# The prologue of a transformer decoder block: loads on two queues, products of ones at the start, v made between the first maximum scores

## The chip, the cores and the metric

The kernel runs on one core of one Trainium2 chip. A core has TensorE (matrix products), VectorE, ScalarE and GpSimd, and SyncE, which here only issues transfers; each takes its own instructions in order, and they meet at semaphores. A transfer can be issued by SyncE, ScalarE or GpSimd and runs on 16 shared DMA engines. The metric is the device time of one execution in microseconds (us), the median of several.

## The reference, cut to what matters

```python
def attn(x, w_q, w_k, w_v, w_o):              # x: 4 x 1024 x 256, 16 heads of 16
    q, k, v = x @ w_q.T, x @ w_k.T, x @ w_v.T # split into heads
    scores = einsum("bqhd,bkhd->bhqk", q, k) * 16 ** -0.5
    return (softmax(scores) @ v) @ w_o.T
x = layernorm(x + attn(x, ...))
x = layernorm(x + cross_attn(x, ctx, ...))    # 77 context rows, one head of 256
x = layernorm(x + moe(x, ...))                # 8 experts 256 -> 1024 -> 256, top 2
```

All is float32. The change touches only the beginning of the first line: q, k and v of batch 0.

## The kernel before

The whole block is one program. Self-attention is done head by head, 64 heads in all (4 batches of 16). For each head there are 8 tiles of 128 rows, and each tile is scored twice: once with the rows across the partitions, to get each row's maximum (`score_max`, into the banks pa; VectorE reduces it in `maxima`), and once turned round, with the negated maxima as three more rows of the contraction, so that ScalarE can take the exponential straight from PSUM (`score_exp`, `exponentials`). The main loop runs over 256 pairs of tiles (`for p in range(PAIRS)`); the maxima run LEAD = 8 pairs, that is two heads, ahead of the exponentials. Side work for the layers behind is spread over the same loop by its number. After it come 71 tiles of the expert layer. The order on each engine is written out by hand, as one stream of instructions for each.

Products with q and k are done in bf16, so each of q and k is split into three bf16 parts, high, middle and low: ScalarE rounds (`first_high`), VectorE subtracts (`first_remainder`), ScalarE rounds again (`first_middle`), VectorE subtracts again (`first_low`). The parts go to DRAM (`store_group`, three transfers for a group) and come back by head, stacked to 96 rows (`load`, three transfers for q and three for k).

The prologue, before the main loop, runs so:
- SyncE issues w_q, w_k, four pieces of x (two column halves, two row halves), w_v, all on its queue.
- TensorE waits for both weights and the first half of x, then makes 8 groups of q and k (`project_qk`, 512 columns each, in the order q, k of column half 0, q, k of half 1, for the first eight heads, and the same for the last eight), then v in 8 products of 256 columns (`project_v`), then 16 maximum scores (heads 0 and 1), then it enters the main loop.
- SyncE stores groups 0 to 3 as their parts come, waits until these have landed, issues twelve loads for heads 0 and 1, stores groups 4 to 7, loads head 2 and x of the next batch, and then sends the negated maxima of head 0 to DRAM (`store_neg`) and back as rows of q's tile (`load_rows`).
- VectorE sets constants (the semaphore set_up counts them), takes its part in the splitting, then does the 16 maxima, and after the 11th (n = TB + 2) turns the negated maxima of head 0 (`turn_neg`), which waits for GpSimd's `split`.
- GpSimd loads the weights of the cross-attention when x is in, then waits for all of v to copy head 0's (`values`), splits the negated maxima of head 0 (`split`), and only then issues the loads of seven constants, wanted some tens of us later.
- ScalarE does its part of the splitting and then copies v out of PSUM (`take_v`).

In the trace, w_sb is the arena of expert weights that the prologue's tiles (q, k, v, the parts) share, attn_t holds x, space holds w_q and w_k, px, po and pb are the four PSUM banks of the projections in turn, and pa the two of the maxima. L886 is `project_qk` and `project_v`, L893 the score products in quarters, L477 the stores of parts, L494 and L495 the loads of q and k parts, L500 and L505 `store_neg` and `load_rows`, L1405 `maxima`, L1412 `turn_neg`, L731 `values`, L740 to L746 `split`, L799 to L805 the constants.

Of the kernel before, what the change touches and what calls it, by code (L numbers as in the profile page):

```python
# [116 lines left out]
def stream(nc, g):  # L117
# [100 lines left out]
    with ExitStack() as st:  # L218
# [130 lines left out]

        w_in, v_in, x_in, x_next = sem("w_in"), sem("v_in"), [sem(f"x_in{c}") for c in range(2)], sem("x_next")  # L350
        const_in, cross_in = sem("const_in"), sem("cross_in")
# [23 lines left out]
        last_back, last_rec, last_rep, last_scaled = (sem(f"last_{n}") for n in ("back", "rec", "rep", "scaled"))  # L375
        picks_made = sem("picks_made")

# [37 lines left out]
        def load_w2(eng, e, f=slice(0, FT)):  # L415
            eng.dma_start(g.w2_sb[:, e, f], g.w2[e][:, f]).then_inc(g.w2_in.sem, 16)

        W2_LOADS = NE + 1
# [41 lines left out]
        with nc.Block() as block:  # L460
            @block.sync
            def _(sp):
# [17 lines left out]
                def load(i):  # L480
                    b, m = divmod(i // PER, KD)
                    if i >= RING:
                        sp.wait_ge(b_done, 2 * TB * (i - RING + 1))
                        settle(sp, g.settled_dma)
                    if i % PER == 0:
                        for which in range(2):
                            if b == 0:
                                sp.wait_ge(first_out[m][which], 96)
                            else:
                                sp.wait_ge(parts_out[which], 48 * (4 * (b - 1) + 3 + m))  # L490
                    at = 0
                    for n in (3, 2, 1):
                        rows = slice(at, at + HD * n)
                        sp.dma_start(qs[i % RING][rows, :], q_dram[i, HD * (3 - n):3 * HD]).then_inc(loaded[i % RING], 16)  # L494
                        sp.dma_start(ks[i % RING][rows, :], k_dram[i, 0:HD * n]).then_inc(loaded[i % RING], 16)  # L495
                        at += HD * n

# [87 lines left out]

                for which, w in enumerate((g.wqT, g.wkT)):
                    sp.dma_start(w_qk[:, which], w.rearrange("(k p) n -> p k n", p=P)).then_inc(w_in, 16)
                for c in range(2):
                    for k in range(KD):
                        sp.dma_start(x0[:, k, c * HALF:(c + 1) * HALF], g.xT[k * P:(k + 1) * P, c * HALF:(c + 1) * HALF]  # L590
                                     ).then_inc(x_in[c], 16)
                sp.dma_start(w_v[:, :, :], g.wvT.rearrange("(k p) n -> p k n", p=P)).then_inc(v_in, 16)
                for i in range(4):
                    store_group(0, i)
                load(0)
                load(1)
                for i in range(4, GROUPS):
# [113 lines left out]
            def _(pool):  # L711
# [84 lines left out]

                values(0)
                split(0)
                pool.dma_start(g.ident[:, :], g.eye).then_inc(const_in, 16)  # L799
# [4 lines left out]
                pool.dma_start(g.woT_sb[:, :, :], g.woT.rearrange("(k p) n -> p k n", p=P)).then_inc(const_in, 16)  # L804
                pool.dma_start(g.b1_sb[:, :], g.b1T).then_inc(const_in, 16)  # L805
                for p in range(PAIRS):
                    i, quarter = divmod(p, HP)
                    turn, s = divmod(p, TURN)
                    j, before = tile_of(p)
                    b = next_batch(p)  # L810
                    if s == 0 and before is not None:
                        spread_2(before)
                    if quarter == 0 and i + 1 < NH:
                        split(i + 1)
                        values(i + 1)
                    if s == 1 and b:
                        lower_parts(b, turn % TB)
                    if s == 3 and j is not None:
                        spread_1(j)
                    n, r = divmod(p, HP * PER)  # L820
                    if n and r == TURN:
                        scale_heads(n - 1)
                    done, since = divmod(turn - DELAY, TB)
                    done -= 1
                    if done >= 0 and s in (2, 3, 5, 6):
                        t = 2 * (2, 3, 5, 6).index(s)
                        if since == 2:
                            scatter_first(done, t)
                            scatter_first(done, t + 1)
                        if since == 3:  # L830
                            if t == 0:
                                reweight(done)
                            scatter_second(done, t)
                            scatter_second(done, t + 1)
# [49 lines left out]
            def _(pe):  # L884
# [183 lines left out]

                pe.wait_ge(w_in, 32)
                pe.wait_ge(x_in[0], 16 * KD)  # L1070
                for i in range(GROUPS):
                    c, m, which = group(0, i)
                    if i == 2:
                        pe.wait_ge(x_in[1], 16 * KD)
                    if i >= 4:
                        pe.wait_ge(first_rest, i - 3)
                    project_qk(whole, banks[i % 4], x0, slice(c * HALF, (c + 1) * HALF), m, which).then_inc(first_made, 1)
                pe.wait_ge(v_in, 16)
                for t in range(TB):
                    if t < 4:  # L1080
                        pe.wait_ge(first_rest, t + 5)
                    else:
                        pe.wait_ge(first_v, t - 3)
                    project_v(whole, banks[t % 4], x0, t * P).then_inc(first_made, 1)
                pe.wait_ge(set_up, SET_UP)
                for n in range(2 * LEAD):
                    score_max(n)
                pe.wait_ge(first_v, TB)
                for p in range(PAIRS):
# [46 lines left out]
                def last_reps():  # L1136

                    pe.wait_ge(picks_made, 4)
                    pe.wait_ge(last_rec, 1)
                    pe.wait_ge(mixed, MAIN_PROJ)  # L1140
# [57 lines left out]
            def _(act):  # L1198
# [75 lines left out]
                def behind(p):  # L1274
# [29 lines left out]
                    if s == 7 and since == 0 and done >= 1:  # L1304
                        gap_exp(done - 1)

                for i in range(GROUPS):
                    first_high(i)
                    if i:
                        first_middle(i - 1)  # L1310
                first_middle(GROUPS - 1)
                for t in range(TB):
                    act.wait_ge(first_made, GROUPS + t + 1)
# [56 lines left out]
            def _(dve):  # L1370
# [274 lines left out]
                def pick_rows():  # L1645

                    dve.wait_ge(crossed, 2 * TB)
                    for j in range(4):
                        own = g.ident[0:4 * PER, 0:4 * PER].rearrange("p (h j o) -> p j h o", j=4, o=1)[:, j]
                        dve.tensor_copy(to_dims[:, j, :].rearrange("p (h d) -> p h d", d=HD),  # L1650
                                        own.to_broadcast([4 * PER, PER, HD])).then_inc(picks_made, 1)

# [86 lines left out]
                for n in range(2 * LEAD):  # L1739
                    maxima(n)  # L1740
                    if n == TB + 2:
                        turn_neg(0)
# [176 lines left out]
```

## Time and profile before

| | us |
|---|---|
| median of 3 runs | 1474.02 (1472.77 to 1474.66) |
| profiled execution | 1476.74 |
| its span in the trace | 1474.9 |
| TensorE busy | 1406.7 (95%) |
| VectorE busy | 974.4 (66%) |
| ScalarE busy | 860.8 (58%) |
| GpSimd busy | 392.7 (27%) |

All times of rows are counted from the start of the span. TensorE holds 84% of the chain of work that ended last, VectorE 8%, transfers 2%, issuing on SyncE 1%. In the page's strip of 40 slices (36.9 us each) TensorE is busy 7 tenths in the first and 9 or more in all others but the last; its clock stands at 9 tenths in the first slice, 7 in the second, and 9 in all others but the last. The prologue is therefore the part to look at closely.

### The profile page before, as it was taken

Reading aid. Unit: us, or ns where it says so; the run is one execution under the profiler, and the core shown is the slowest. Engines: PE = TensorE matmul, PEld = TensorE weight load, DVE = VectorE, ACT = ScalarE, POOL = GpSimd, SP = SyncE. Lnnn points to the kernel's source line nnn. Section 1 sums busy time; section 2 is a strip of 40 time slices with the busy share of each in tenths; the row PEclk is TensorE's granted clock in tenths of the full one; section 3 lists DMA queues with packets and bytes.
Section 4 is the critical chain, followed back from the end, with each engine's and each line's share of the span. In section 5 each row is a group of like instructions: output and inputs, shape, how many; then the busy total and the mean of one; then the engine's idle time right before and its main releaser. Section 6 shows DMA issues by size and latency. Waiting matters only on the chain.

```text
span 1474.9 us, 47861 instructions
## 1 busy us (share of the span) xinstructions
PE 1406.7 (95%) x18586; PEld 928.3 (63%) x18586; DVE 974.4 (66%) x1685; ACT 860.8 (58%) x1966; POOL 392.7 (27%) x676
## 2 busy tenths in 40 slices
PE   7999999999999999999999999999999999999990
PEld 3354445444444545444444458889999999999980
DVE  6777788888888888888988954656333333333326
ACT  3477788887777777778878783333333333333320
POOL 1211121212212215321225211455422222222223
PEclk9799999999999999999999999999999999999995
DMA  4324232334434323322433242224322222222216
GB/s 159 95 70 137 67 92 89 109 115 135 129 98 133 113 81 113 105 80 74 133 92 106 77 166 65 66 78 105 78 37 37 37 37 37 38 37 41 40 19 232
DMA packets 104840, 130.99 MB, mean 89 GB/s; under 512 B 25770, under 2 KB 81370, under 8 KB 103594
## 3 DMA queue, kind: packets, MB, share of 16 engines
q1 hardware_dynamic: 89322, 103.74, 23.3%
q0 software_dynamic: 14000, 19.48, 7.4%
q10 hardware_dynamic: 1296, 4.72, 0.8%
q8 instruction: 150, 2.46, 0.7%
q14 instruction: 72, 0.59, 0.1%
HBM read 75.98 MB, written 51.90 MB: 87 GB/s over the span
## 4 chain that ended last, share of the span: by engine, by line
PE 84%; DVE 8%; issue 3%; DMA 2%; ACT 1%; SPq 1%; POOL 0%; DVEq 0%; POOLq 0%; ACTq 0%
PE pa L1116 17%; PE pb L1130 16%; PE pa L893 14%; PE pb L893 13%; PE po L1063 13%; PE px L893 7%; DVE neg L1405 4%; PE px L886 2%; PE po L992 1%; ACT w_sb L1219 1%; PE px L967 1%; PE px L942 1%; DVE w_sb L1864 1%; DMA x<-space,y_tags 1%; SPq L477 0%
## 5 line engine op out<-in xcount | busy, mean ns | idle before, releaser
L1219 ACT ACTIVATE w_sb<-pb 128x512 f32<-128x512 f32 x996 | 590.0, 599 | 137.7 <-PE pb L893 102.8
L1405 DVE TENSOR_REDUCE neg<-pa 128x1 f32<-128x1024 f32 x512 | 612.0, 1213 | 87.2 <-PE pa L893 80.0
L893 PE MATMUL pb<-w_sb 99*32 99x512 bf16 x3984 | 393.4, 381 | 6.0 <-DMA w_sb<-minus_maxima 3.1
L1335 ACT ACTIVATE space<-pa,b1T_sb 128x128 f32<-128x128 f32 x568 | 154.7, 383 | 318.4 <-PE pa L1116 318.4
L893 PE MATMUL pa<-w_sb 96*32 96x512 bf16 (+1 forms) x4208 | 328.1, 385 | 11.6 <-DVE neg L1405 10.9
L1063 PE MATMUL po<-w_sb,space 128*32 128x256 f32 x4000 | 304.6, 379 | 0.0
L1116 PE MATMUL pa<-xgT,attn_t 128*128 128x128 f32 x2272 | 268.9, 275 | 0.4 <-DVE attn_t L1717 0.4
L1116 PEld LDWEIGHTS pa<-xgT,attn_t 128*128 128x128 f32 x2272 | 266.1, 192 | 4.9 <-issue 1.4
L1130 PE MATMUL pb<-w_sb,space 128*128 x1136 | 260.4, 380 | 0.0
L1130 PEld LDWEIGHTS pb<-w_sb,space 128*128 128x128 f32 x1136 | 208.8, 190 | 25.2 <-issue 0.3
L844 POOL DMA_INDIRECT x<-space,y_tags x71 | 116.9, 1647 | 366.8 <-DVE space L1782 299.5
L893 PEld LDWEIGHTS pa<-w_sb 96*32 96x32 bf16 (+1 forms) x4208 | 102.5, 97 | 135.7 <-DVE neg L1405 38.3
L1063 PEld LDWEIGHTS po<-w_sb,space 128*32 128x32 f32 x4000 | 123.3, 111 | 100.5
L893 PEld LDWEIGHTS pb<-w_sb 99*32 99x32 bf16 x3984 | 106.1, 95 | 121.7 <-ACT w_sb L1219 16.8
L1717 DVE COPY attn_t<-w_sb 128x1024 f32 x142 | 100.0, 706 | 89.9 <-PE pa L1116 86.9
L1778 DVE TENSOR_TENSOR space<-pb,b_sb 128x256 f32<-128x256 f32 x71 | 30.1, 424 | 179.5 <-PE pb L1130 172.9
L740 POOL TENSOR_TENSOR neg_parts<-neg,ones 128x8 bf16<-128x8 f32 x64 | 13.1, 204 | 236.7 <-DVE neg L1405 236.7
L775 POOL TENSOR_TENSOR dev_B<-mv_B,eps 128x1 f32<-128x1 f32 x32 | 8.4, 263 | 232.7 <-DVE mv_B L1469 232.7
L893 PE MATMUL px<-w_sb,space 128*32 128x512 f32 x384 | 47.1, 611 | 0.0
L784 POOL DMA_INDIRECT x_by_expert<-pay,pos_i x32 | 33.3, 1040 | 14.4 <-issue 10.3
L794 POOL DMA_INDIRECT x_by_expert<-pay,pos_i x32 | 32.7, 1021 | 11.4 <-issue 7.8
L731 POOL TENSOR_TENSOR space<-w_sb,ones 128x128 f32<-128x128 f32 x64 | 29.4, 459 | 18.2 <-ACT w_sb L1208 17.3
(226 smaller groups left out, 973.9 us busy)
## 6 DMA issues: line engine op xcount, KB each, us to landing
xg<-x_by_expert SPq DMA_DIRECT2D x71, 130.0 KB, 2.5
w_sb<-w SPq DMA_DIRECT2D x17, 512.0 KB, 5.3
attention_out<-space SPq DMA_DIRECT2D x64, 128.0 KB, 2.1
w_sb<-w SPq DMA_DIRECT2D x7, 1024.0 KB, 8.0
q_parts<-w_sb SPq DMA_DIRECT2D x48, 128.0 KB
w_sb<-q_parts SPq DMA_DIRECT2D x64, 96.0 KB, 2.6
w_sb<-k_parts SPq DMA_DIRECT2D x64, 96.0 KB, 2.7
k_parts<-w_sb SPq DMA_DIRECT2D x45, 128.0 KB
```

The costliest lines, as they stand in the source:

```text
L784: pool.indirect_dma_start(g.xe_dram, bass.IndirectOffsetOnAxis(pos_i[b % 2][:, 0, t:t + 1], 0), pay[b % 2][:, t, :], None, bounds_check=X_ ...
L794: pool.indirect_dma_start(g.xe_dram, bass.IndirectOffsetOnAxis(pos_i[b % 2][:, 1, t:t + 1], 0), pay[b % 2][:, t, :], None, bounds_check=X_ ...
L844: pool.indirect_dma_start(g.x2_dram, bass.IndirectOffsetOnAxis(y_tag[tile % TAGS][:, 0:1], 0), y[tile % 2], None, bounds_check=Y_ROWS - 1, ...
L893: mm = pe.matmul(out[at:end], lhsT[:, at:end], rhs, start=start, stop=stop, tile_position=(0, at))
L1063: mm = pe.matmul(po[32 * j:32 * j + VW, 0:QC], vs[i % 2][:, t, :], ex_of(n)[:, j * QC:(j + 1) * QC], start=t == 0, stop=t == TB - 1, tile_ ...
L1116: mm = pe.matmul(pH[tile % 2][:, f, :], w1_e[:, k, f * P:(f + 1) * P], xgT[tile % 2][:, k, :], start=k == 0 and f % PER_BANK == 0, stop=k ...
L1130: mm = pe.matmul(pY[tile % 2], hT[tile % 2][:, f, :], g.w2_sb[:, bass.ds(e, 1), f, :].rearrange("p e d -> p (e d)"), start=f == 0, stop=f ...
L1219: act.activation(ex_of(n)[:, half * HALF:(half + 1) * HALF], score_bank(n, half), ACT.Exp, scale=SCALE).then_inc(e_done, 1)
L1335: ins = act.activation(hT[tile % 2][:, f, :], pH[tile % 2][:, f, :], ACT.Relu, bias=g.b1_sb[:, bass.ds(e * FT + f, 1)])
L1405: dve.tensor_reduce(neg[i % 2][:, t:t + 1], pa[n % 2][:, :], AX.X, ALU.max, negate=True).then_inc(max_done, 1)
L1717: dve.tensor_copy(w1_e[:, k], g.w1_sb[:, bass.ds(e, 1), k].rearrange("p e f -> p (e f)")).then_inc(w1_copied, 1)
L1778: dve.tensor_tensor(y[tile % 2], pY[tile % 2], b2_sb[:, bass.ds(e, 1), :].rearrange("p e d -> p (e d)"), ALU.add).then_inc(raw_done, 1)
```

## The change

1. Loads on two queues: SyncE issues w_q, the first row half of both pieces of x, and w_v; ScalarE issues the second row halves and w_k. TensorE waits for w_q before group 0 and for w_k before group 1.
2. TensorE begins with twelve products of ones (128x128, float32) into a bank that is overwritten later.
3. The k parts of heads 0 and 1 are loaded by ScalarE, behind its part of the splitting and ahead of the copies of v; the q parts by SyncE.
4. v is no longer made between the projections and the scores: each of the first eight maximum scores is followed by one product of v.
5. VectorE turns the first negated maxima after the 9th maximum (n = TB), not the 11th.
6. GpSimd issues the loads of the constants after the first maximum, ahead of `values(0)` and `split(0)`.
7. The semaphore picks_made is merged into last_rec, which the same instructions raise.

```diff
@@ sync
+        def load_parts(eng, i, which):
+            at = 0
+            for n in (3, 2, 1):
+                rows = slice(at, at + HD * n)
+                if which == 0:
+                    eng.dma_start(qs[i % RING][rows, :], q_dram[i, HD * (3 - n):3 * HD]).then_inc(loaded[i % RING], 16)
+                else:
+                    eng.dma_start(ks[i % RING][rows, :], k_dram[i, 0:HD * n]).then_inc(loaded[i % RING], 16)
+                at += HD * n
...
-                for which, w in enumerate((g.wqT, g.wkT)):
-                    sp.dma_start(w_qk[:, which], w.rearrange("(k p) n -> p k n", p=P)).then_inc(w_in, 16)
+                load_w_qk(sp, 0)
                 for c in range(2):
-                    for k in range(KD):
-                        sp.dma_start(x0[:, k, c * HALF:(c + 1) * HALF], g.xT[k * P:(k + 1) * P, c * HALF:(c + 1) * HALF]
-                                     ).then_inc(x_in[c], 16)
+                    load_first_x(sp, c, 0)
                 sp.dma_start(w_v[:, :, :], g.wvT.rearrange("(k p) n -> p k n", p=P)).then_inc(v_in, 16)
                 for i in range(4):
                     store_group(0, i)
-                load(0)
-                load(1)
+                for which in range(2):
+                    sp.wait_ge(first_out[0][which], 96)
+                for i in range(2):
+                    load_parts(sp, i, 0)
                 for i in range(4, GROUPS):
                     store_group(0, i)
@@ gpsimd
-                values(0)
-                split(0)
+                pool.wait_ge(max_done, 1)
                 pool.dma_start(g.ident[:, :], g.eye).then_inc(const_in, 16)
...
                 pool.dma_start(g.b1_sb[:, :], g.b1T).then_inc(const_in, 16)
+                values(0)
+                split(0)
@@ tensor
-                pe.wait_ge(w_in, 32)
+                pe.wait_ge(set_up, 1)
+                for _ in range(12):
+                    whole(banks[1][:, 0:P], g.ones[:, :], g.ones[:, :], True, True)
                 pe.wait_ge(x_in[0], 16 * KD)
                 for i in range(GROUPS):
                     c, m, which = group(0, i)
+                    if i < 2:
+                        pe.wait_ge(w_in[which], 16)
...
+                pe.wait_ge(set_up, SET_UP)
                 pe.wait_ge(v_in, 16)
-                for t in range(TB):
-                    if t < 4:
-                        pe.wait_ge(first_rest, t + 5)
-                    else:
-                        pe.wait_ge(first_v, t - 3)
-                    project_v(whole, banks[t % 4], x0, t * P).then_inc(first_made, 1)
-                pe.wait_ge(set_up, SET_UP)
                 for n in range(2 * LEAD):
                     score_max(n)
+                    if n < TB:
+                        if n < 4:
+                            pe.wait_ge(first_rest, n + 5)
+                        else:
+                            pe.wait_ge(first_v, n - 3)
+                        project_v(whole, banks[n % 4], x0, n * P).then_inc(first_made, 1)
@@ scalar
+                load_first_x(act, 0, 1)
+                load_w_qk(act, 1)
+                load_first_x(act, 1, 1)
                 for i in range(GROUPS):
                     first_high(i)
                     if i:
                         first_middle(i - 1)
                 first_middle(GROUPS - 1)
+                for which in range(2):
+                    act.wait_ge(first_out[0][which], 96)
+                for i in range(2):
+                    load_parts(act, i, 1)
                 for t in range(TB):
                     act.wait_ge(first_made, GROUPS + t + 1)
                     take_v(banks[t % 4], 0, t, first_v)
@@ vector
                 for n in range(2 * LEAD):
                     maxima(n)
-                    if n == TB + 2:
+                    if n == TB:
                         turn_neg(0)
```

## Rows read from the trace of the kernel before

**Rows 1.** The chain that ended last, 0 to 70 us: start, us, what.
```profile
2.26 4.81 DMA attn_t<-xT
...
10.95 2.47 PE po L886 x4
...
15.38 0.74 SPq L477
...
22.83 3.86 DMA k_parts<-w_sb
26.76 0.35 SPq L494
...
27.62 0.42 SPq L494
...
29.02 1.79 DMA w_sb<-k_parts
...
30.94 0.64 PE pa L893 x8
...
44.72 3.94 DMA minus_maxima<-neg_turned
48.68 1.42 DMA w_sb<-minus_maxima
...
50.23 0.64 PE pb L893 x4
```

**Rows 2.** TensorE's timeline, 0 to 62 us: start, us, instruction, count [idle before].
```profile
16.68 1.88 PE L886 MATMUL px<-attn_t,space 128*128 128x512 f32 x4
...
23.55 1.03 PE L886 MATMUL px<-w_sb,attn_t 128*128 128x256 f32 x4
...
39.88 2.20 PE L893 MATMUL pa<-w_sb 96*32 96x512 bf16 x16 [0.18 <-DVE neg L1405]
...
48.23 1.04 PE L893 MATMUL pa<-w_sb 96*32 96x512 bf16 x8 [0.18 <-DVE neg L1405]
```

**Rows 3.** Busy time by stretch, projection products alone: stretch, length, PE, PEld, clock, DMA.
```profile
7.20:12.30 5.10, 5.10 (x6) 2.14 (x7) 1.00 0.38 125
```

**Rows 4.** Busy time by stretch, TensorE alone: stretch, length, busy (count), granted clock.
```profile
30.90:36.20 5.30, 2.89 (x40) 1.00 0.46 144
36.20:48.00 11.80, 10.40 (x80) 0.50 0.70 220
```

**Rows 5.** Busy time by stretch, all engines: PE PEld DVE ACT POOL, clock, DMA.
```profile
56.00:57.00 1.00, 1.00 (x16) 0.21 (x12) 0.00 (x0) 0.04 (x1) 0.00 (x0) 0.66 0.00 0
```

**Rows 6.** TensorE's timeline in the expert layer, 128x128 f32 products at full clock.
```profile
1105.31 3.73 PE L1116 MATMUL pa<-xgT,attn_t 128*128 128x128 f32 x32
```

**Rows 7.** VectorE's timeline, 0 to 62 us.
```profile
0.83 0.17 DVE L1719 MEMSET ones<- 128x128 f32 x1 [0.83 <-PEq L1912]
...
31.61 12.97 DVE L1405 TENSOR_REDUCE neg<-pa 128x1 f32<-128x1024 f32 x11 [3.19 <-PE pa L893]
```

**Rows 8.** ScalarE's timeline, 0 to 62 us.
```profile
30.66 0.37 ACT L1208 COPY w_sb<-pb 128x256 f32<-128x256 f32 x1 [0.49 <-PE pb L886]
```

**Rows 9.** GpSimd's timeline, 0 to 62 us.
```profile
31.18 0.45 POOL L731 TENSOR_TENSOR space<-w_sb,ones 128x128 f32<-128x128 f32 x1 [17.32 <-ACT w_sb L1208]
41.05 0.21 POOL L740 TENSOR_TENSOR neg_parts<-neg,ones 128x8 bf16<-128x8 f32 x1 [9.42 <-DVE neg L1405]
...
42.05 0.59 POOL L799 DMA_DIRECT2D ident<-eye  x1
...
45.67 0.59 POOL L805 DMA_DIRECT2D b1T_sb<-b1T  x1
```

**Rows 10.** SyncE's timeline, 0 to 62 us: its issues of transfers.
```profile
43.03 0.90 SPq L557 DMA_DIRECT2D w_sb<-xT  x2
...
59.55 0.52 SPq L500 DMA_DIRECT2D minus_maxima<-neg_turned  x1
61.47 0.24 SPq L505 DMA_DIRECT2D w_sb<-minus_maxima  x1
```

More of the change, by code:

```diff
@@ L347, in stream @@
         pY = [pb[i][:, 0:D] for i in range(2)]
-        w_in, v_in, x_in, x_next = sem("w_in"), sem("v_in"), [sem(f"x_in{c}") for c in range(2)], sem("x_next")
+        w_in, v_in, x_in, x_next = [sem(f"w_in_{n}") for n in "qk"], sem("v_in"), [sem(f"x_in{c}") for c in range(2)], sem("x_next")
         const_in, cross_in = sem("const_in"), sem("cross_in")
@@ L375, in stream @@
         last_back, last_rec, last_rep, last_scaled = (sem(f"last_{n}") for n in ("back", "rec", "rep", "scaled"))
-        picks_made = sem("picks_made")
         projected, turned_1, scored, p_turned, crossed, turned_2, gated, ranked = (
@@ L416, in load_w2, with load_first_x, load_w_qk @@
             eng.dma_start(g.w2_sb[:, e, f], g.w2[e][:, f]).then_inc(g.w2_in.sem, 16)
+        def load_parts(eng, i, which):
[7 more added lines that the diff above has]
+                at += HD * n
+        def load_first_x(eng, c, k):
+            eng.dma_start(x0[:, k, c * HALF:(c + 1) * HALF], g.xT[k * P:(k + 1) * P, c * HALF:(c + 1) * HALF]
+                          ).then_inc(x_in[c], 16)
+        def load_w_qk(eng, which):
+            eng.dma_start(w_qk[:, which], (g.wqT, g.wkT)[which].rearrange("(k p) n -> p k n", p=P)).then_inc(w_in[which], 16)
         W2_LOADS = NE + 1
@@ L490, in load @@
                                 sp.wait_ge(parts_out[which], 48 * (4 * (b - 1) + 3 + m))
[L491 to L496, printed above, removed]
+                    for which in range(2):
+                        load_parts(sp, i, which)
                 def store_neg(i):
@@ L1136, in last_reps @@
                 def last_reps():
-                    pe.wait_ge(picks_made, 4)
-                    pe.wait_ge(last_rec, 1)
+                    pe.wait_ge(last_rec, 4 + 1)
                     pe.wait_ge(mixed, MAIN_PROJ)
@@ L1311, in _ @@
                 first_middle(GROUPS - 1)
+                for which in range(2):
+                    act.wait_ge(first_out[0][which], 96)
+                for i in range(2):
+                    load_parts(act, i, 1)
                 for t in range(TB):
@@ L1650, in pick_rows @@
                         dve.tensor_copy(to_dims[:, j, :].rearrange("p (h d) -> p h d", d=HD),
-                                        own.to_broadcast([4 * PER, PER, HD])).then_inc(picks_made, 1)
+                                        own.to_broadcast([4 * PER, PER, HD])).then_inc(last_rec, 1)
                 def pads():
```

## The prediction

> **What bounds the kernel now.** The page comes first: TensorE is busy 95% of the span and holds 84% of the chain that ended last. From about 57 us on it works through a fixed order of products almost without a gap, so what happens before that can only shift the rest, and I count such a shift one for one. The change touches only the start, so the second view is the chain of waits for the first 51 us [rows 1]. It is hardly TensorE at all: loads of x until 7.07 (2.26 + 4.81); two projection groups until 13.42; the split into three bf16 parts until SP can store the first part at 15.38; SP's own issuing of twelve stores until 22.83; their landing (3.86) at 26.69; SP's issuing of loads for head 0, of which six are needed (the sixth starts at 29.02) and 1.79 for the last to land; the first score product at 30.94; maxima on VectorE; and the negated maxima through DRAM and back (3.94 + 1.42), so that the first exponential's scores start at 50.23. **That start, 50.23, is the number I follow.** The last of the sixteen score products before it starts at 48.23 and hands over about 0.86 later, at 49.1 [rows 2], so the round trip of the maxima costs some 1.1 us there.
>
> The third view is the clock. A row of the projection shows 6 instructions in 5.10 us at first [rows 3], 0.85 each, against 1.72 for four, 0.43 each, later [rows 2]: the first 5.1 us of work ran at 1.2 GHz, the rest at 2.4 (the granted column says 1.00 there, the durations decide). While only maxima are made, TensorE is busy 2.89 of 5.30 us, then the granted clock falls to 0.50 [rows 4] and is back within 56 to 57 us, at 56.68 by the mean of 0.66 [rows 5].
>
> **Part by part, up to the first score.** (1) Loads. Group 0 now needs w_q and both pieces of x, w_k is awaited one group later, and ScalarE issues one piece of x first. SP's chain had two more issues of about 0.5 ahead of the x piece that ended last. The least gain is 0, the most 1.6, if the bytes left out of the need (256 of 1024 KB) counted fully and issue also shrank. Since the same bytes still share one set of transfer engines, I take 0.5: first projection at 6.7 instead of 7.20. A table load may run on ScalarE ahead of its issues; that is one of the reasons not to take more.
> The Trainium skill, "DMA: Bandwidth & Descriptors", section "Issuing engines are not separate DMA queues", states that issuing from several engines only saves the sequencers' time. By it the 0.5 would be near 0 and my forecast 0.5 later, within the range.
> (2) Twelve products of ones. A 128x128 f32 product is two instructions; 32 of those take 3.73 us at full clock less the drain of one [rows 6], 0.11 each, so 0.22 at half clock by the ratio of 0.85 to 0.43. 24 x 0.22 = 5.2 us from about 1.1 (the memset of ones ends at 1.00 [rows 7]) to 6.3. They end before 6.7 and cost nothing if the loads land no earlier; if x landed at 5.5 they would cost 0.8. They last as long as the 5.1 us after which the clock rose before, so the projections should run at full speed: two groups in 3.54 instead of 6.22 (13.42 less 7.20), 2.7 saved. Ends: 0 saved if the clock does not rise, 2.7.
> (3) The chain behind is unchanged to the landing of the stores: 13.42 to 15.38 is 1.96, and SP's twelve issues plus landing, 15.38 to 26.69, is 11.31 [rows 1]. Group 3's parts are ready at 6.7 + 5 x 1.72 + 1.96 = 17.3, before SP comes to them, so SP stays the bound. So 6.7 + 3.54 + 1.96 + 11.31 = 23.5.
> (4) Loads of the heads' parts. Third instead of sixth issue: the third starts 0.86 after the first (26.76 to 27.62) instead of 2.26, and the landing is 1.79, so 2.75 with the small steps instead of 4.12: 1.4 saved (0 if two engines' issues got in each other's way). ScalarE must be through its eight groups: 6.7 + 13.8 + some 2 = 22.5, so it is not late. **First score product at 23.5 + 2.75 + 0.13 = 26.4, instead of 30.94: 4.5 earlier.**
> (5) v is moved. Before, groups end where v begins, 23.55 [rows 2], and eight products of v (256 columns, half of a group, 0.86 each) fill TensorE to 30.4; left there it would now end at 20.5 + 6.9 = 27.4 and be the bound. Its 6.9 us now stand behind the first eight score products. At full clock a pair is 0.43 + 0.86 = 1.29 against 1.18 of a maximum (12.97 for 11 [rows 7]): TensorE becomes the bound for eight steps, 26.4 + 10.3 = 36.7 to product 8, 0.9 more than maxima alone. ScalarE's copy of v takes 0.37 [rows 8] and hides.
> But between 20.5 and 26.4 TensorE has nothing to do, 5.9 us, while before it kept its clock only until 36.20, 5.3 after the thin stretch began [rows 4]. So I expect half clock at 26.4. A pair is then 2.58, which is dense work, and dense work brought the clock back after 5.1 us at 7.20 and 6.45 us at 50.23 [rows 3, 5]. Half of that time is lost: 2.6 to 3.2. **Product 8 at about 39.4** (before: 39.88 [rows 2]). This is where most of the 4.5 us goes.
> (6) The negated maxima. turn_neg(0) moves from behind maximum 10 to behind maximum 8, and GpSimd's split in front of it waits in turn for values(0), which waits for the last v. The last v is copied 0.6 after product 8 starts; values takes 0.45, the split 1.0 (41.05 to 42.05 [rows 9]), so it ends 2.2 after. Maximum 8 ends 1.8 after. VectorE therefore stands in turn_neg with maxima 9 to 15 queued behind it, and TensorE behind those: 0.6 with the transpose. Product 8 itself runs 0.6 closer to maximum 7 than in the steady cadence, so the distance to product 15 stays 8.35 (39.88 to 48.23). 39.4 + 8.35 + 0.86 = **48.6**.
> Does the round trip still end later? Stored from 41.8, and 3.94 + 1.42 and the small steps give 47.3; in a quiet stretch the way took 1.9 (59.55 to 61.47) [rows 10]. It is hidden, with at least 1.3 to spare. SP is free for it: all its work from 26.76 to 43.93 [rows 1, 10] now starts 3.3 earlier and is six issues (2.8) shorter, free at 37.9.
> (7) The constants, seven issues from 42.05 to 45.67 plus 0.59 [rows 9], move behind maximum 0: about 28 to 32, GpSimd then waits until 40 anyway. Were it not idle they would cost their 4.2. They collide with the second four groups' stores, which nobody awaits before 48. The merged semaphore has the same releasers as before: nothing. After 48.6 the clock is again at half, as before at 50.23, and comes back after as long a time; no difference there.
>
> **The sum.** 50.23 less 48.6 is 1.6 earlier. On the profiled execution (span 1474.9, time 1476.74) that is 1473.3 and 1475.1; that execution lies 2.7 over the median, so on the median, 1474.02 gives **1472.4**.
>
> **Rivals.**
> A. The clock is not lost in the gap, or is back at once. For: the fall at 36.20 came 5.3 us into a thin stretch, about as long as the gap. Against: that stretch was half busy, this one is empty. Then product 8 is at 36.7, exponentials at 45.9, the round trip at 44.6: 4.3 earlier, 1469.7.
> The Trainium skill, "TensorE: Matmul & The Clock Gate", section "HAM oscillation — how this bites in real kernels", describes the opposite: waits for data that let the clock drop, with the next stretch starting slow; moving v behind the wait would feed it that way. By it my forecast holds and A is excluded.
> B. Slower: v between the maxima is done wholly at half clock. From 36.20 to 48.00 TensorE was busy 10.40 of 11.80 and stayed at 0.50 [rows 4], so nearly full is not enough. Eight pairs are 20.6: product 8 at 47.0, exponentials at 56.2, 6.0 later, 1480.0. It decides from the point where 8.6 us after 26.4 have gone by at half clock (half of them lost, 4.3: the forecast's 2.7 and its gain of 1.6). Against it: pairs leave no gap at half clock.
> C. The start does not do what it says: the ones end, a pause follows and projections run slow (2.7 lost). The first score is at 29.1, the exponentials at 51.3 at most, 1.1 later: 1475.1.
>
> **How the numbers follow.** Forecast 0.58, its own range 1470.8 to 1473.8 (the loads from 0 to 1.1 and the clock's return by 1 either way). A 0.22, B 0.11, C 0.09. The range for all is 1469.0 to 1475.3: it holds the forecast, C and most of A, and leaves B out. A measurement of this kernel can tell about 0.2%, 2.9 us. Faster by more: A and the early end of the forecast, 0.22 + 0.58 x 0.2 = 0.34. Slower by more: 0.09, nearly all of B. Within: 0.57.
>
> **What would show it.** Right: first full-speed projection before 7.2 and 0.43 per instruction from the first; first score product near 26.4; granted clock 0.50 around it and 1.00 again near 32; product 8 near 39.4; a gap of about half a microsecond in VectorE ahead of the first transpose; scores for the first exponential near 48.6 and behind the last maximum, not behind the load of minus_maxima. The prediction is wrong if the clock never falls there (A), stays down (B), or if the stretch after 57 us does not simply shift.

## The result and the profile after

| | before | changed |
|---|---|---|
| median, 6 runs each | 1473.12 (1471.93 to 1474.66) | 1480.08 (1478.21 to 1482.09) |
| profiled execution, span | 1476.74, 1474.9 | 1479.53, 1477.4 |

The changed kernel is **slower: 1.0048 times before, 95% interval 1.0035 to 1.006, about 7 us**. The two profiled executions are only 2.5 us apart in span, because the one of before lies 3.6 over its median and the one of the changed kernel 0.6 under its own; so a trace can tell here where time goes, but not alone how much. In what follows the start of the first exponential's scores is always read from TensorE's own timeline; the chain of waits, which merges pieces, can show it about 0.2 later.

The chain of waits of the changed kernel is the counterpart of [rows 1] (start, us, what):

```profile
1.25 5.83 DMA attn_t<-xT
...
7.13 1.98 PE px L899 x4
...
20.86 3.85 DMA k_parts<-w_sb
...
25.68 3.39 DMA w_sb<-k_parts
...
29.21 1.04 PE pa L906 x8
30.25 2.01 PE px L899 x4
...
34.29 0.55 PE pa L906 x8
34.84 1.06 PE pb L899 x4
35.90 0.55 PE pa L906 x8
...
45.93 0.21 DVE neg_turned L1436
46.14 5.64 DVE neg L1429 x5
...
51.83 1.04 PE pa L906 x8
52.87 0.46 PE pb L906 x4
```

The projections run at full clock from their first instruction (1.98 for four, against 3.75 before) and start at 7.13 instead of 7.20. The last piece of x that is needed was issued 1.01 earlier and landed at the same time (7.08, before 7.07). The first score starts at 29.21, only 1.7 before the old one. Of the eight pairs of one score and one product of v, the first two are slow, 2.98 and 2.03 up to 34.22, and each further one takes 1.61 = 0.55 + 1.06. Product 8 starts at 43.86, and the first exponential's scores at 52.66 (in the chain above 52.87), **2.4 later than the old 50.23**.

TensorE alone, by stretch (length, busy, granted clock), is the counterpart of [rows 4]:

```profile
22.00:26.00 4.00, 0.00 (x0) 1.00 0.36 106
26.00:33.00 7.00, 3.79 (x20) 0.52 0.73 203
33.00:36.00 3.00, 3.00 (x24) 0.98 0.71 211
36.00:46.00 10.00, 9.10 (x80) 1.00 0.62 175
```

A granted clock of 0.50 is 1.2 GHz, 1.00 is 2.4 GHz, so the means put the fall at about 26.3, in the pause, and the return at about 33.1: it was at half for the first 3.9 us of work. It falls once more, at 50.2, and stays at half until 60.4, which is 7.8 behind the first exponential's scores; before, it was back 6.45 behind them.

```profile
50.00:60.00 10.00, 9.03 (x68) 0.51 0.11 29
```

The second part of the loss is far from the change. What TensorE waited for between 66 and 880 us in a second profile of the changed kernel (f1, below; us in total, times, longest):

```profile
PE pa L906 <- DVE neg L1429: 6.3, 15, 0.7
PE pb L906 <- DMA w_sb<-minus_maxima: 3.8, 1, 3.8
```

The one wait of 3.8 us is at head 6, near 135 us. SyncE's queue in that profile, ahead of it:

```profile
113.84 0.57 SPq L523 DMA_DIRECT2D attention_out<-space  x1
115.22 0.24 SPq L518 DMA_DIRECT2D w_sb<-minus_maxima  x1
117.57 0.32 SPq L539 DMA_DIRECT2D attn_t<-attention_out  x1
...
119.11 10.14 SPq L669 DMA_DIRECT2D x<-attn_t  x15
129.43 1.25 SPq L423 DMA_DIRECT2D w_sb<-q_parts  x3
130.73 2.70 SPq L425 DMA_DIRECT2D w_sb<-k_parts  x3
133.47 0.54 SPq L513 DMA_DIRECT2D minus_maxima<-neg_turned  x1
```

SyncE stores the attention output of head 3 (`attention_out`) at 113.84 and cannot go on before this store has landed, at 117.57. Then, at head 4, it issues fifteen stores of spare rows into x2 in one block of 10 us. Head 6's negated maxima stand behind it. **SyncE, which in other heads waits for the others, is for this once on the path**, so the stretch after 57 us does not simply shift with the start, which was the premise of my sum. The trace of the kernel before already had this block on SyncE and the wait of TensorE behind it:

```profile
115.89 10.46 SPq L657 DMA_DIRECT2D x<-attn_t  x15
PE pb L893 <- DMA w_sb<-minus_maxima: 2.2, 1, 2.2
```

In the first profile of the changed kernel the same wait is 3.2:

```profile
PE pb L906 <- DMA w_sb<-minus_maxima: 3.2, 1, 3.2
```

### The profile page after: what moved, and what is told of

Same layout as the page of the kernel before. It is cut to its first block, busy times and chain, and to the rows that moved or that the text cites. A ratio compares the mean times of both kernels' runs of the same rounds, so it can differ in the third digit from the quotient of the medians.

```text
span 1477.4 us, 47909 instructions
## 1 busy us (share of the span) xinstructions
PE 1408.3 (95%) x18610; PEld 934.2 (63%) x18610; DVE 974.2 (66%) x1685; ACT 861.2 (58%) x1966; POOL 391.7 (27%) x676
## 4 chain that ended last, share of the span: by engine, by line
PE 83%; DVE 8%; issue 3%; DMA 2%; ACT 1%; SPq 1%; POOL 0%; DVEq 0%; POOLq 0%; ACTq 0%
PE pa L1134 17%; PE pb L1148 16%; PE pa L906 14%; PE pb L906 12%; PE po L1076 12%; PE px L906 7%; DVE neg L1429 4%; PE px L899 2%; PE po L1005 1%; ACT w_sb L1236 1%; PE px L980 1%; PE px L955 1%; SPq L669 1%; DVE w_sb L1888 1%; PE pb L899 1%
## 5 line engine op out<-in xcount | busy, mean ns | idle before, releaser
L779 POOL TENSOR_TENSOR dev_A<-mv_A,eps 128x1 f32<-128x1 f32 x32 | 6.7, 210 | 101.9 <-DVE mv_A L1455 101.9
```

## The experiments

Theory V: v between the scores costs the time. Theory S: SyncE's block of fifteen stores sets the time of head 6. Theory I: where in the run TensorE's program is fetched decides how late that block is. Runs were made on several chips; each ratio is to the kernel before on the same chip, with its 95% interval. On two of the chips (e and g below) the kernel before took 1499 and 1500 us instead of 1474.

**e1: the kernel before, unchanged.**

> The kernel before, unchanged, as a second profiled execution and as the measure of how far two sets of runs of one kernel differ. The profiled execution of before stood 3.6 us over the median of its six runs. If that was chance in a late stretch, this profile has a span near 1471, the first exponential's scores again near 50.2, and the missing 3 us behind that. If the start itself varies (the clock), the first exponential's scores move by more than 1 us.

Ratio 0.9997 [0.9987, 1.0008]. The first exponential's scores start at 51.28, since x landed at 8.02 instead of 7.07. Its wait at head 6 is 1.4. So the start varies by 1 us. This profile is 21.8 longer than the one of before, and nearly all of it arises between 560 and 830 us, where VectorE has waits that the view calls "remote"; the first profile of before has none:

```profile
DVE neg L1405 <- remote: 17.1, 5, 4.0
```

**e2: v ahead of the scores again.** ScalarE copies four of v, issues the k loads, copies the rest.

```diff
                 for n in range(2 * LEAD):
                     score_max(n)
-                    if n < TB:
...
-                        project_v(whole, banks[n % 4], x0, n * P).then_inc(first_made, 1)
```

> The changed kernel with its v products put back between the projections and the scores (ScalarE copies four of v, issues the k loads, copies the other four). Theory V, that v between the scores is what costs (pairs of 1.61 and a lost clock): the first score product at 29.2 as in the changed kernel, then maxima every 1.18, the first exponential's scores at 47.4 instead of 52.7; 5 us faster than the changed kernel and 2.8 faster than before, about 1470.5. Rival L, that the loads on two queues and SyncE's order cost and v is innocent: within 1 us of the changed kernel, 1479 to 1480.

Ratio 0.9998 [0.9989, 1.0008]. The prologue did what theory V says: the first score starts at 28.58 and the first exponential's scores at 46.72 (46.94 in the chain), 4.6 before those of e1.

```profile
28.58 0.64 PE pa L906 x8
...
46.94 0.45 PE pb L906 x4
```

But the time is that of before, which neither V (2.8 faster) nor L (6 slower) had. By TensorE and stretch, the gain is given back at head 6: a pause, then a stretch at half clock.

```profile
127.00:131.00 4.00, 1.04 (x20) 1.00 0.23 63
131.00:134.00 3.00, 2.67 (x40) 0.78 0.29 84
134.00:137.00 3.00, 3.00 (x28) 0.65 0.70 194
```

The exponentials of head 6 are 2.4 earlier than in e1 at their first and 0.7 at their fifth. A lead at 50 us says little about the end. (The profiled execution of e2 lies 2.8 over its median, so its span proves nothing by itself.)

**e3: only v moved, the rest as before.**

> The kernel before with only the v products moved between the first eight maximum scores. Theory V: TensorE idles from 23.5 to 30.9, two pairs at half clock, six at 1.61, product 8 at 45.6, the first exponential's scores near 54.5; 4 to 5 us slower than before, about 1478. Rival L: pairs are hidden behind something else and the time is within 1 us of before.

Ratio 1.0023 [1.0013, 1.0033], 3.4 us. The first exponential's scores start at 54.3, as expected, 3.0 after those of e1. Of this 2.3 are left at the 61st maximum, 1.9 behind head 6, and the spans are 3.2 apart. So v's place costs 3 us by itself, a little less than the 4 to 5 expected.

**e4: only the loads on two queues and the ones.**

> The kernel before with only the loads on two queues and the twelve products of ones. Theory V: projections at 7.1 and at full clock, v ends at 27.8, the heads' loads land at 28.8, the first exponential's scores at 48.2 (the round trip of the maxima ends last); 2 us faster than before, about 1471. Rival L: slower than before by 1 us or more, or not faster, because the queue order hurts later.

Ratio 1.0012 [1.0002, 1.0023]: not faster, although the first exponential's scores start at 47.85. It waits 4.2 at head 6, with the granted clock at 0.50 behind it. The expectation of theory V held for the prologue and failed for the time. The time is the one of rival L, but not by its reason, the second queue: h3 below has one queue and loses as much (1.0014).

**f1: the changed kernel again**, with f2 to f4 beside it on one chip.

> The changed kernel, unchanged, for a second profile on another chip and as the partner of the runs beside it. Theory S (SyncE's sixteen stores of spare rows in one block, issued in about 10 us ahead of the loads and negated maxima of head 6, set the time of head 6): first exponential's scores near 52.7, TensorE then idle 2 to 4 us for minus_maxima near 135, and if that pause is over 3 us a drop of the clock to 0.50 behind it; 5 to 7 us slower than before. Rival P (the loss lies in the prologue alone, and the later stretch only shifts): 2 to 3 us slower than before.

Ratio 1.0041 [1.0027, 1.0055]; wait 3.8, and the granted clock is 0.62 on average from 137 to 140 us. As theory S has it.

**f2: the block spread over eight heads.**

```diff
-                        for e in range(NE + SPARE):
+                    if 4 <= i < 12:
+                        for e in range(2 * (i - 4), min(2 * (i - 3), NE + SPARE)):
```

> The changed kernel with the fifteen stores of spare rows into x2 spread over eight heads, two for each, instead of one block at head 4; all are still awaited at head 12. Theory S: no wait of TensorE for minus_maxima at head 6 and no drop of the clock there, so 3 to 5 us faster than the changed kernel, 2 to 3 slower than before. Rival P: as fast as the changed kernel within 1 us.

Ratio 1.0009 [0.9999, 1.0018]: 1475.11 against 1479.84 of f1, **4.7 us faster by moving stores that the change never touched**. TensorE no longer waits for minus_maxima at head 6. Its lead over f1 arises there: f2 is 0.7 later than f1 at the 61st maximum and 5.0 earlier at the 67th. Rival P falls.

**f3: v first and the block spread.**

> v between the projections and the scores, loads on two queues, ones, and the stores of spare rows spread. Theory S: the 4.5 us gained at the first exponential last to the end and the wait of before (1.4 to 2.2) goes too: 5 to 6 us faster than before. Rival G (the gain is given back by something else, such as the engines' order in the main loop): within 2 us of before.

Ratio 0.9971 [0.9959, 0.9982], 1469.34 against 1473.59 of before: 4.3 us faster, a little less than expected. Against f2 it is 5.8 faster, by v's place and the order on ScalarE that goes with it (the k loads stand between the fourth and fifth copy of v). The lead is 5.9 at the first exponential and 5.5 at the 61st maximum, and here, without a block, it lasts (5.4 at the 501st). It is more than the 3.4 of e3, in part because there v's place also let the first score start 1.3 earlier than in e1 (here 0.5) and hid a wait of 1.2 for the negated maxima (here there is none).

**f4: the kernel before, block spread.**

> The kernel before with only the stores of spare rows spread. Theory S: the wait of 1.4 to 2.2 us at head 6 goes, and 1 to 2 us with it. Rival G: no difference.

Ratio 0.9998 [0.9989, 1.0007]. A miss: the wait goes from the trace, but the median does not move. The kernel before loses nothing measurable to the block in its median; the changed one does. The two traces alone would have said otherwise (2.4 gained at head 6), which is why medians decide here.

**g1: f2 with v in quarters** (`project_v(quarters, ...)`).

> The changed kernel with the stores of spare rows spread (f2) and the v products between the scores made in quarters of 32 columns, as the score products are. Theory Q, that the change of the products' shape between scores and v costs 0.32 in each pair (1.61 measured, 0.43 + 0.86 = 1.29 worked out): pairs of 1.29 at full clock and 2.58 at half, the first exponential's scores 1.9 earlier than in f2, 2 us faster than f2. Rival W, that the pair waits for something else (PSUM, weights): pairs stay at 1.6 and the time is that of f2 within 0.5 us.

Ratio 1.0003 [0.9994, 1.0012], 0.6 thousandths under f2 on another chip, within both intervals: the 2 us expected in the time are not to be seen. The pairs are settled by TensorE's timeline, though: score to score is 1.30, and the first exponential's scores start at 50.46 instead of 53.18.

```profile
35.04 0.61 PE L907 MATMUL pa<-w_sb 96*32 96x512 bf16 x8
35.48 1.04 PE L907 MATMUL pb<-w_sb,attn_t 128*32 128x256 f32 x16
36.34 0.61 PE L907 MATMUL pa<-w_sb 96*32 96x512 bf16 x8
```

So 0.31 of each pair of 1.61 was the change of form, twice a pair, and rival W falls.
The Trainium skill says this in "TensorEngine Tiling (Array Packing)", section "Key Properties": changing the tiling mode drains TensorE. The rows agree, at about 0.16 a change; the prediction did not use this rule.

**g2: f3 with the loads of head 1 issued later.**

> f3 (v ahead of the scores, all else of the change, stores of spare rows spread) with the loads of head 1 issued later, so that six and not twelve loads are in flight when the first score waits. If the 3.2 to 3.4 us of landing come from twelve transfers sharing the engines, the last k part lands 1.8 us after its issue and the first score starts 1.4 us earlier, the time 1 to 1.4 us lower than f3 (about 1468). If the two queues as such are slow, the landing stays over 3 us and nothing is gained.

Ratio 0.9966 [0.9953, 0.9979]. The first score starts at 27.96, straight behind v and 1.1 before that of f3 (29.05). The third k load, issued at 25.41, was in by then, at most 2.6 later, against 3.4 in f3, so the six loads needed land sooner when the other six are not yet issued. In time it can't be told from f3: the 1 to 1.4 us expected are within the noise.

**g3: f3 without the ones.**

> f3 without the twelve products of ones. If they give the clock, the first 5 us of projections run at 0.85 per instruction, the first parts are stored 2.5 to 2.7 later and the time is 2.5 us over f3. If they give nothing, the same as f3.

Ratio 0.9993 [0.9984, 1.0003], 2.2 thousandths or 3 us over f3. The first four instructions of the projections take 3.75 again, as expected. The ones are worth having in this kernel.

**g4: f2 with TensorE's pause filled by ones.**

> The changed kernel with the stores of spare rows spread (f2) and 28 products of ones in TensorE's pause between the projections and the first score. If the clock lost in the pause costs what the first pairs show (2.98 each instead of 1.61), all eight pairs take 1.61, the first exponential's scores start 2.5 to 3 earlier than in f2 and the time is 2 to 3 us below f2, about that of before. If the clock is no part of it, the time is that of f2.

Ratio 1.0003 [0.9994, 1.0013]. All pairs take 1.61 and the first exponential's scores start at 50.95 instead of 53.18 of f2, 2.2 earlier where 2.5 to 3 were expected. In the time the 2 to 3 us are not to be seen: a miss. It adds 112 instructions to TensorE, which by h1 to h4 can move the time by itself, so what the fill is worth stays open.

**What was still open** was why the wait at head 6 is 3.2 to 4.2 with the new start (changed kernel, f1, e2, e4) and 1.0 to 2.2 with the old (before, e1, e3). In f1 the store of attention_out for head 3 is issued at 113.84 and SyncE goes on at 117.57, 3.7 later. The transfers of that stretch of f1:

```profile
q8 instruction: 1, 0.02, 2.1%
...
attention_out<-space SPq DMA_DIRECT2D x1, 128.0 KB, 3.6
```

A transfer of the queue "instruction" (16 KB of program) is in flight with the store. I take it to be TensorE's program: this queue makes 150 or 151 such transfers in each of the 18 profiles, one for every 256 to 257 recorded instructions of TensorE (38,579 in the kernel before), and no other engine records more than 3,643. They come near the same places when TensorE's instructions are counted, so 48 instructions put in front bring each one about 48 instructions of the program earlier. Over the 14 profiles up to g4 there are 882 stores of attention_out for heads 0 to 62: of the 336 that met such a fetch (in flight at some time from 0.8 to 2.0 us after the issue) 69% held SyncE over 2.5 us, of the other 546 10%. For the store of head 3 the two groups do not overlap, h1 to h4 included: 3.35 to 4.05 in the eight profiles with a fetch (the changed kernel, e2, e4, f1, f2, f3, g2, h3), 1.96 to 2.15 in the ten without.
The Trainium skill, "Advanced Engine Details and Errata", section "ISA Cache", gives a line of 16 KB, 256 instructions, for the programs. The transfers' size agrees; the 48 instructions of the ones are a fifth of a line.

**h1: the changed kernel, ones in 3 products of 512 columns instead of 12 of 128.**

```diff
-                for _ in range(12):
-                    whole(banks[1][:, 0:P], g.ones[:, :], g.ones[:, :], True, True)
+                wide_ones = g.ones[:, :].rearrange("p (o n) -> p o n", o=1).to_broadcast([P, 4, P])
+                for _ in range(3):
+                    whole(banks[1][:, :].rearrange("p (o n) -> p o n", o=4), g.ones[:, :], wide_ones, True, True)
```

> The changed kernel with the twelve products of ones of 128 columns made as three of 512: the same work and time, 36 instructions of TensorE fewer. Theory I (the 48 instructions of the ones move the points at which TensorE's program is fetched, the fetch of 16 KB then meets the store of attention_out of head 3 just ahead of SyncE's block, and the block starts some 2 us late): that store lands after 2.0 instead of 3.7 to 4.0 us, TensorE waits 2.2 us or less for minus_maxima at head 6, the clock does not drop there, and the time is 2 to 3 us under the changed kernel, a ratio to before near 1.002. Rival E (the earlier start or the second queue brings the wait): landing and wait as in the changed kernel, ratio 1.004 to 1.005.

Ratio 1.0017 [1.0007, 1.0027] against 1.0041 and 1.0048 of the changed kernel, as theory I said. SyncE's queue in h1 is that of f1 to within 0.1 us from about 75 us up to the same store, and then:

```profile
113.93 0.51 SPq L523 DMA_DIRECT2D attention_out<-space  x1
...
115.91 0.32 SPq L539 DMA_DIRECT2D attn_t<-attention_out  x1
...
117.45 10.22 SPq L669 DMA_DIRECT2D x<-attn_t  x15
127.85 1.62 SPq L423 DMA_DIRECT2D w_sb<-q_parts  x3
129.51 1.35 SPq L425 DMA_DIRECT2D w_sb<-k_parts  x3
130.91 0.54 SPq L513 DMA_DIRECT2D minus_maxima<-neg_turned  x1
```

The store holds SyncE 1.98 instead of 3.73 and meets no fetch, the k loads take 1.35 to issue instead of 2.70 (a fetch falls there too in f1), and the negated maxima leave 2.6 earlier. TensorE waits 1.2 instead of 3.8 and keeps its clock (1.00 from 134 to 140). From the 21st maximum up to head 6 the two traces are 0.1 apart, behind it h1 is 4.2 ahead: 2.6 by the maxima and 1.6 by the clock that was kept.

**h2: the same for e2.**

> The same for the kernel with v ahead of the scores (e2, ratio 0.9998). Theory I: the store of head 3 lands after 2.0, the wait at head 6 is 2 us or less with no drop of the clock, and 3 of the 4.5 us gained at the start last: ratio 0.998. Rival E: wait of 3.3 us and drop of the clock as in e2, ratio 1.000.

Ratio 0.998 [0.997, 0.9989], as expected; wait 1.5, no drop of the clock.

**h3 and h4: the kernel before with the ones alone**, in twelve products and in three.

> The kernel before with only the twelve products of ones in front (48 instructions), loads on one queue. Theory I: projections at full clock, the first exponential's scores 2.5 us earlier, but the store of head 3 lands after 3.4 to 4.0 us, TensorE waits over 3 us at head 6, and the time is within 1.5 us of before. Rival E (the second queue at fault): wait of 1 to 2 us, 2 us faster than before.

> As h3 with three products of 512 columns (12 instructions). Theory I: the store of head 3 lands after 2.0, the wait at head 6 is 2 us or less, 2 to 3 us faster than before and than h3. Rival E: the same time as h3.

Ratios 1.0014 [1.0005, 1.0023] and 0.9987 [0.9978, 0.9995], on one chip: 1477.49 and 1472.89. **The same work in 36 instructions fewer is 4.6 us faster, and turns a loss into a gain.** Both sizes were missed: h3 was to be within 1.5 of before and is 2 to 3 slower, h4 was to be 2 to 3 faster than both and is 1.5 to 1.9 faster than before. The place was in part another than expected: the store of head 3 held SyncE 3.4 in h3, but TensorE waited only 2.0 at head 6 (0.7 in h4). Of 3.9 us that h3's trace is behind h4's after head 6, 2.6 are there before it. In h3 a fetch already met the loads of head 1,

```profile
30.13 1.55 SPq L495 DMA_DIRECT2D w_sb<-k_parts  x1
```

where such an issue takes 0.42 elsewhere. SyncE was then busy until 43.34 with what came before the negated maxima, which took 5.14 to land, and the scores started at 50.06, in h4 at 47.05. Only 1.1 of these 3.0 are the slow issue; x landed 0.85 later in h3, which its instructions do not explain, and why the maxima took so long to land was not tested. The profiled execution of h3 (1474.61) is also the fastest of its eleven, 2.9 under their median, so its trace does not show the typical loss. That 36 instructions fewer are worth 4.6 us here is shown; that fetches are the whole reason is argued from h1 and h2.

**Where the delays arise.** All 512 maxima are in every trace, so two traces can be compared at the same instruction. Difference of start in us, worked out from the kept traces; the exponentials of head 6 begin beside the 65th maximum:

| | 21st | 61st | 67th | 301st | 501st |
|---|---|---|---|---|---|
| changed less before | 2.95 | 2.95 | 4.01 | 4.05 | 2.57 |
| f1 (changed again) less before | 1.89 | 1.90 | 5.22 | 5.26 | 4.07 |
| f2 less f1 | 0.62 | 0.66 | -5.03 | -5.11 | -5.80 |
| h1 less f1 | 0.10 | 0.08 | -4.21 | -4.26 | -3.65 |
| h3 less h4 | 2.60 | 2.59 | 3.90 | 3.88 | 2.81 |

The drop in the last column of the first two rows is a property of the one profile of before: near 800 us its TensorE waits 4.4 for maxima, the changed kernel's 3.0. That is part of why it lies over its median. So the traces place 4 to 5 of the 6 to 7 us, in the prologue and at head 6, and the rest is in the medians alone.

## Why the prediction was wrong, step by step

Two steps failed: the sum up to the first exponential, and what the rest of the kernel makes of it.

- **The sum to the first exponential's scores** said 48.6, 1.6 earlier than 50.23. The trace has 52.66, 2.4 later. Passed on one for one, that alone gives 1475.5 to 1476.5 by the two medians of before (1473.12 and 1474.02), slower and already past the range. Its wrong terms are parts 4 and 5 below.
- **"I count such a shift one for one"** failed as well: the time is 7 longer, not 2.4. f2 shows 4.7 of the 6 to 7 to be SyncE's block at head 4, which costs the kernel before nothing measurable (f4), and h1 about 3.5 of that to go when 36 instructions of TensorE go. No rival had this: they were all inside the first 57 us. The prediction did name a stretch that "does not simply shift" among its signs of being wrong, but gave it no price and no chance, though the trace of before showed TensorE waiting 2.2 at head 6.
- Part 1, loads: the first projection 0.1 earlier, not 0.5, and x landed no earlier. The rule of the Trainium skill cited there ("DMA: Bandwidth & Descriptors", section "Issuing engines are not separate DMA queues") had put the gain near 0; the trace agrees.
- Part 2, ones: as worked out (1.05 to 6.25, full clock from the first projection). What their 48 instructions cost elsewhere was put at nothing, without a reason.
- Part 3: stores landed at 24.71, 0.8 over the sum apart from the late start; 0.6 of it is slower issuing by SyncE (8.06 from the first to the last issue, not 7.45).
- Part 4, loads by two engines: 4.50 from landing to first score, not 2.88. The issue did come earlier, but with all twelve loads issued within 2.8 us the third k load takes 3.39 to land instead of the 1.79 taken from before: the 1.4 expected was lost. g2 points the same way.
- Part 5: pairs at full clock cost 1.61, not 1.29, by the change of form (g1): 2.6 over eight pairs. The fall of the clock was right in place and its return near 32 only 1 us off (33.1), but since the first score came late, only 3.9 us of work ran at half clock and the loss was 1.8, not 2.7. Product 8 stands 14.65 after the first score, not 13.0. v's place costs 3.4 us alone (e3).
- Part 6: VectorE's stop and the distance to the exponentials were right: 8.8 from product 8, not 9.2, the round trip hidden. "No difference there" for the clock behind the exponentials was not: it came back 7.8 behind them instead of 6.45, and the delay grew from 2.45 to 2.95.
- The terms together: 2.8 (first score at 29.21 instead of 26.4: 0.4 start, 0.8 stores, 1.6 loads), 1.65 (2.6 change of form less 0.9 clock), less 0.4, make 52.66 out of 48.6. Rival B had the direction, and its 1480.0 met the measured 1480.08 by luck: the clock came back after two pairs, and the exponentials were 2.4 late and not 6.0.
- The range left out every case in which the rest does not shift with the start, and its upper end also the case of a prologue that is slower.

What stays open: the kernel before waits 1.4 to 2.2 at head 6 in two profiles, and yet gains nothing from f4. How a fetch lengthens a store is not shown, only that it goes with it and goes away with it. And 1 to 3 of the 6 to 7 us are placed by no trace.

**The better version.** f3 (0.9971) and g2 (0.9966) beat both kernels: the change's start, v left ahead of the scores, and the block of stores spread. h2 (0.998) has the fewer instructions instead of the spreading. Both together were not run.

## What to carry to other kernels

A gain at the start is worth its size only if nothing between it and the end keeps a time of its own: look in each queue, SyncE's above all, for the longest block that does not wait for the engine you sped up, and see who stands behind it. Keep products of different forms apart rather than alternating them (0.16 us a change here), and leave work that fills a pause where it is. Count instructions, not only microseconds, in work that is put in "for free", and compare two versions by a kernel that differs in the number of instructions alone before a change of 0.3% is believed.

## What the runs showed of the hardware

- The transfers of 16 KB on the queue "instruction" come once in 256 to 257 recorded instructions of TensorE (all 18 profiles). One in flight with a store goes with a longer landing: attention_out 3.6 instead of 1.9 (f1, h1), and single issues on SyncE of 1.55 instead of 0.42 (h3).
- A change between products of 128 columns and quarters of 32 costs TensorE about 0.16 us each way (1.61 against 1.30 a pair).
- Behind TensorE's waits of 3.3, 3.8 and 4.2 us at head 6 (e2, f1, e4) the granted clock stood at half for a while (means over 3 us of 0.65, 0.62 and 0.50); behind the wait of 3.2 in the first profile of the changed kernel it stayed at 1.00. In e2 the drop took 1.7 us more (a lead of 2.4 became 0.7).
- The same kernel took 1473 to 1474 us on some chips and 1499 to 1500 on two others, with most of the difference between 560 and 830 us, where VectorE's waits stand (17.1 us in five of them in e1, none in the first profile of before).
